# A graph layer summed over half blocks of 128 edges in place of blocks of 256

## The chip, the cores and the metric

One core of a Trainium2 chip runs the whole program. The metric is the device time of one execution in microseconds (us).

## The reference

Four layers follow each other on 3125 nodes with 256 values each: a graph layer over 103,125 edges (three steps), a mixture of experts, a second graph layer over the same edges with 500 relation kinds, and a second mixture of experts. The change is in the second graph layer. The edges come sorted by their target `dst`. Cut to what matters here:

```python
h_src = h_hc[src]                       # one row of 256 values for each edge
r_uv  = r_hc[edge_type]                 # its relation's row
m = clifford_linear(h_src * r_uv, msg_w, msg_b)
m = m * gate[:, :, None] * norm[:, None, None]
h_agg = segment_sum(m, dst, num_segments=num_nodes)
```

Since the linear map is the same for all edges, the kernel sums the products `h_src * r_uv` (already scaled by gate and norm, with the scale itself as column 257) over the edges of a target first, and applies the map to the 3125 sums afterwards.

## The kernel before

The sum is made by `aggregate` (L547). The nodes stand in 25 tiles of 128 (`NT`), and `acc` holds one [128, 257] float32 tile of sums for each, with a 26th as a bin for what belongs to nobody. The 103,424 edge rows are cut into 404 blocks of 256 (`BLOCKS`), in order of `dst`. A block begins in one tile of nodes, whose number is in the table `b_tile`; edges of a block that belong to the next tile are dealt with by 24 more blocks (`EDGES_AT`), one for each border between two tiles: the block in which tile j begins is taken once more with j as its tile. So `total` is 428 blocks.

For each block n, in slot n % 12 (`SLOTS`):

- SP loads the 256 relation rows (L594), 2 rows to a partition, 2080 contiguous bytes each. `relation_rows` was written by earlier stages.
- POOL gathers the 256 rows of `h_table` by two indirect DMAs of 128 rows (L608), with the row numbers in `b_src`. SP and POOL wait until the sum of block n-12 is made, and so run up to 12 blocks ahead.
- ACT makes two one-hot matrices [128 edges, 128 nodes] from `b_near` (L575 twice, L578), in `BANKS` = 6 buffers.
- DVE's queue reads the tile number into a register (L637, `value_load`), DVE multiplies gathered rows by relation rows (L629, 128x514), then adds the sum of block n-3 (`LAG` = 3) from its PSUM bank to `acc[tile]` (L623).
- PE multiplies one-hot by rows, for both halves into one bank (L657): `start` on the first, `stop` on the second, four matmul records of 128x257 in the profile for a block.

Semaphores set the order: `s_sum` counts finished sums (from 13), `s_acc` counts additions (from 6), `s_ready` multiplications, `s_oh` one-hot pairs. The queue of each engine is in the order of the code. DVE's loop is

```python
block_of(n): wait s_rel, s_rows of the slot; multiply; then add(n)
add(g): wait s_acc >= g + BANKS; wait s_sum >= g + (SLOTS + 2 - LAG); addition; s_acc += 1
```

Beside this, `Beside` (L2283) does small work for each of the 25 node tiles, every 14th block from n = 48 on: four transposes and matmuls on PE, a copy on ACT, two additions on DVE (L2365, L2367).

The tables `b_src`, `b_near`, `b_tile` and `b_start` are made early in the program by `edge_blocks` (L361), beside the first relation rows' fetch and store (POOL and ACT's queue, `RelationRows`), and are loaded again much later. `edge_blocks` transposes the edge lists with PE (L465) and picks the 24 border blocks with small matmuls (L470).

## Time and profile before

| | |
|---|---|
| median of 3 runs | 3487.85 us |
| lowest, highest | 3473.99, 3497.01 us |
| the profiled execution's time | 3479.88 us |
| its span, first to last instruction | 3478.1 us |
| mean granted TensorE clock in it | 0.840 |
| busy share PE, DVE, ACT, POOL | 72%, 39%, 41%, 58% |
| DMA moved | 620.94 MB, mean 179 GB/s |

The span is what the trace shows; 1.8 us of the execution lie around it. The busy shares are means over stages that differ in what limits them. The stage of the change runs from 1764 to 2901 us of the span, a third of it. Times in the rows are microseconds from the span's start unless marked ns. Register, branch and semaphore instructions of an engine's queue ("DVEq", "SPq") are not counted as busy.

### The profile page before, as it was taken

How to read it: one execution, taken by the hardware profiler on the slowest of the kernel's cores; microseconds unless marked ns; L12 is line 12 of the kernel's file. 1: busy time of each engine (PE TensorE's matmuls, PEld its weight loads, DVE VectorE, ACT ScalarE, POOL GpSimd, SP SyncE). 2: the span in 40 equal slices, each digit the busy share in tenths (PEclk: the TensorE clock that was granted, in tenths of full speed). 3: DMA queues.
4: the chain of work that ended last, by engine and by line, in shares of the span. 5: the costliest groups of instructions: out<-in, count | busy, mean ns of one | idle time of the engine just before them, and what ended most of it. 6: DMA issues, size and time to landing. Idle time of an engine off the chain costs nothing. (4 is left out here: it accounts for less than half of the span.)

```text
span 3478.1 us, 51218 instructions
## 1 busy us (share of the span) xinstructions
PE 2500.1 (72%) x14080; PEld 1914.7 (55%) x14080; DVE 1343.8 (39%) x4118; ACT 1441.6 (41%) x3690; POOL 2011.4 (58%) x1969
## 2 busy tenths in 40 slices
PE   0156899999999947887036666666666667499997
PEld 0123666678888836776024444444444445488986
DVE  4166889952221142000643444444444435500100
ACT  0025666647650022332354444444444443255553
POOL 0353777777777226663657777777777772033332
PEclk9998999999999958998557667666766768699998
DMA  2574766678888335565367777777777772364232
GB/s 112 191 251 126 209 202 206 206 226 257 269 257 244 123 119 186 181 208 171 104 186 203 202 198 202 202 205 204 206 203 201 205 201 61 124 179 131 37 84 62
DMA packets 314743, 620.94 MB, mean 179 GB/s; under 512 B 82206, under 2 KB 128685, under 8 KB 309777
## 3 DMA queue, kind: packets, MB, share of 16 engines
q1 hardware_dynamic: 207409, 343.11, 30.1%
q0 software_dynamic: 101360, 268.76, 29.2%
q10 hardware_dynamic: 5728, 6.11, 0.5%
q8 instruction: 115, 1.88, 0.2%
q14 instruction: 131, 1.07, 0.1%
HBM read 451.74 MB, written 170.90 MB: 179 GB/s over the span
## 5 line engine op out<-in xcount | busy, mean ns | idle before, releaser
L608 POOL DMA_INDIRECT agg_r_rows<-h_table,parts_and_x x856 | 869.1, 1015 | 296.1 <-issue 218.8
L657 PE MATMUL agg_r_sums<-agg_r_rows,agg_r_onehot 128*128 128x257 f32 x1712 | 703.2, 559 | 389.8 <-DVE agg_r_rows L629 343.6
L657 PEld LDWEIGHTS agg_r_sums<-agg_r_rows,agg_r_onehot 128*128 128x128 f32 x1712 | 430.4, 275 | 645.4 <-issue 581.5
L1412 POOL DMA_INDIRECT rl_buf<-r_table,kinds x608 | 634.4, 1043 | 249.3 <-issue 170.4
L629 DVE TENSOR_TENSOR agg_r_rows<-agg_r_rows,agg_r_rel 128x514 f32<-128x514 f32 x428 | 298.5, 697 | 657.6 <-DMA agg_r_rows<-h_table,parts_and_x 655.6
L575 ACT ACTIVATE agg_r_gap<-iota,parts_and_x 128x128 f32<-128x128 f32 x856 | 295.1, 392 | 496.5 <-PE agg_r_sums L657 470.9
L1782 PE MATMUL f_pH<-f_xT,f_w 128*128 128x128 f32 x2816 | 359.4, 287 | 74.5 <-DMA f_w<-in_L_ffn_w 52.9
L1782 PEld LDWEIGHTS f_pH<-f_xT,f_w 128*128 128x128 f32 x2816 | 343.8, 201 | 106.2 <-DMA f_w<-in_L_ffn_w 57.7
L1134 PE MATMUL ly_acc<-parts,matrix 128*128 128x256 bf16 x1250 | 342.0, 274 | 0.0
L1133 PE MATMUL ly_acc<-parts,matrix 128*128 128x256 bf16 x1250 | 340.2, 272 | 0.0
L1132 PE MATMUL ly_acc<-parts,matrix 128*128 128x257 bf16 (+1 forms) x1250 | 340.0, 272 | 0.0
L1867 ACT ACTIVATE f_hT<-f_pH,f_b 128x128 f32<-128x128 f32 x704 | 197.6, 372 | 333.7 <-PE f_pH L1782 333.4
L1801 PE MATMUL f_pY<-f_w,f_hT 128*128 128x256 f32 x1408 | 327.7, 383 | 0.0
L1801 PEld LDWEIGHTS f_pY<-f_w,f_hT 128*128 128x128 f32 x1408 | 262.0, 193 | 31.4
L2020 POOL DMA_INDIRECT f_xb<-xn_table,f_token x120 | 118.8, 990 | 240.0 <-DVE f_home L1968 116.3
L1270 DVE TENSOR_SCALAR b_oh<-b_numbers,b_code 128x400 bf16<-128x400 f16 x980 | 255.0, 324 | 0.0
L2008 POOL DMA_INDIRECT f_ys<-f_yb,f_home x56 | 88.2, 1575 | 284.3 <-DVE f_yb L1993 242.2
L1121 PE MATMUL b_strips<-b_oh,b_at 128*128 128x400 bf16 x980 | 201.0, 336 | 59.5 <-DVE b_oh L1270 53.5
L1412 POOL DMA_INDIRECT f_rr_buf<-r_table,kinds x120 | 121.4, 1012 | 150.9 <-POOLq L113 112.9
L578 ACT ACTIVATE agg_r_onehot<-agg_r_gap 128x256 f32<-128x256 f32 x428 | 178.2, 416 | 13.5
L623 DVE TENSOR_TENSOR acc<-acc,agg_r_sums 128x257 f32 (+1 forms) x431 | 179.1, 416 | 9.9 <-PE agg_r_sums L657 9.9
L1134 PE MATMUL ly_acc<-parts_and_x,matrix 128*128 128x256 bf16 x625 | 170.6, 273 | 0.0
(394 smaller groups left out, 3404.2 us busy)
## 6 DMA issues: line engine op xcount, KB each, us to landing
agg_r_rel<-relation_rows SPq DMA_DIRECT2D x428, 260.0 KB, 3.0
relation_rows<-rl_buf SPq DMA_DIRECT2D x304, 260.0 KB, 4.5
f_w<-in_L_ffn_W SPq DMA_DIRECT2D x28, 1024.0 KB, 5.0
f_w<-in_L_ffn_w SPq DMA_DIRECT2D x38, 512.0 KB, 5.8
relation_rows<-f_rr_buf POOLq DMA_DIRECT2D x60, 260.0 KB, 2.8
agg_r_rows<-h_table,parts_and_x POOLq DMA_INDIRECT x856, 3.4
ly_zin<-zh SPq DMA_DIRECT2D x50, 256.0 KB, 4.8
zh<-ly_out SPq DMA_DIRECT2D x50, 256.0 KB, 2.7
```

What stands on the lines that cost most here:

```text
L575: last = nc.scalar.activation(gap[:, n % BANKS, t, :], c.iota[:, 0:P], ACT.Abs, bias=c.tab["b_near"][:, bass.ds(g * 2 + t, 1)])
L608: pool.indirect_dma_start(rows[:, n % SLOTS, t, :], None, table, bass.IndirectOffsetOnAxis(ap=indices[:, t:t + 1], axis=0)).then_inc(s_row ...
L629: v.tensor_tensor(here, here, rel[:, n % SLOTS, :, 0:used], ALU.mult).then_inc(s_ready, 1)
L657: last = nc.tensor.matmul(sums[:, n % BANKS, 0:used], onehot[:, n % BANKS, t, :], rows[:, n % SLOTS, t, 0:used], start=t == 0, stop=t == 1)
L1121: last = nc.tensor.matmul(strips[:, n % BANKS, 0:CODES], at[:, n % 2, t, :], oh[:, n % 2, t, :], start=t == 0, stop=t == DEEP - 1)
L1132: nc.tensor.matmul(acc[:, n % 2, 0:D + one], m[:, s, own], of[:, s, 2 * D:3 * D + one], start=s == 0, stop=False)
L1133: nc.tensor.matmul(acc[:, n % 2, 0:D], m[:, s, own], of[:, s, 0:D], start=False, stop=False)
L1134: last = nc.tensor.matmul(acc[:, n % 2, 0:D], m[:, s, own], of[:, s, D:2 * D], start=False, stop=s == NT - 1)
L1270: last = v.tensor_scalar(oh[:, n % 2, t, :], numbers[:, :], code[:, q, 1, own, t:t + 1], None, ALU.is_equal)
L1412: pool.indirect_dma_start(self.buf[:, n, g, :], None, self.table, bass.IndirectOffsetOnAxis(ap=self.c.kinds[:, at:at + 1], axis=0)).then_i ...
L1782: last = nc.tensor.matmul(pH[s][:, f * P:(f + 1) * P], w1b[:, s, h, f * P:(f + 1) * P], xT[:, s, h, :], start=h == 0, stop=h == KD - 1)
L1801: last = nc.tensor.matmul(pY[s][:, 0:D], hT[:, s, f, :], w2b[:, s, f, :], start=f == 0, stop=f == FC - 1)
```

## The change

A half block of 128 edges becomes the unit of the tables, of the one-hot base, of the PSUM bank and of the addition. There are 808 halves, each with a tile number of its own, and 24 halves more for the borders, two of which make one block: `total` is 404 + 12 = 416. Each half's matmul goes to a bank of its own, and DVE adds two banks for each block, with two tile numbers read after the multiplication. Six banks hold three blocks, `LAG` is 2 blocks; the one-hot buffers keep their number, 6 (`HOT`). The relation rows of a block are loaded 128 rows to each half: 1040 contiguous bytes for each partition and half; for the last 12 blocks there are two loads with a start each. `edge_blocks` makes the tables in the new form. Left out of the diff: renamed buffers, and the shapes of tables where they are declared and loaded.

```diff
-SLOTS, BANKS, LAG = 12, 6, 3
+SLOTS, BANKS, LAG, HOT = 12, 6, 2, 6
+HALVES, PER_HALF = 2 * BLOCKS, 2 * PER_PART
@@ edge_blocks: vector
-                v.tensor_scalar(at[:, 0, :], starts, block_bits, block_bits, ALU.arith_shift_right, ALU.logical_shift_left)
+                v.tensor_scalar(at[:, 0, :], starts, bits, bits, ALU.arith_shift_right, ALU.logical_shift_left)
...
-                for b in range(PER_PART):
+                for b in range(PER_HALF):
                     last = v.tensor_scalar(pick[:, b, :], own[:, :], float(b), None, ALU.is_equal)
...
-                for q in range(2):
-                    v.tensor_copy(src_out[:, BLOCKS:, q], extra[:, q * 32:q * 32 + EDGES_AT])
-                    last = v.tensor_tensor(near_out[:, BLOCKS:, q], shift[:, :], extra[:, 64 + q * 32:64 + q * 32 + EDGES_AT], ALU.subtract)
-                last.then_inc(s_out, 1)
+                v.tensor_copy(src_out[:, HALVES:], extra[:, 0:EDGES_AT])
+                v.tensor_tensor(near_out[:, HALVES:], shift[:, :], extra[:, 32:32 + EDGES_AT], ALU.subtract).then_inc(s_out, 1)
@@ edge_blocks: tensor
-                for q in range(4):
-                    for b in range(PER_PART):
-                        last = nc.tensor.matmul(extra[:, q * 32:q * 32 + EDGES_AT], both[:, q // 2, b, q % 2:BLOCK:2], pick[:, b, :],
-                                                start=b == 0, stop=b == PER_PART - 1)
+                for q in range(2):
+                    for b in range(PER_HALF):
+                        last = nc.tensor.matmul(extra[:, q * 32:q * 32 + EDGES_AT], both[:, q, b, :], pick[:, b, :],
+                                                start=b == 0, stop=b == PER_HALF - 1)
@@ aggregate
-    total = BLOCKS + EDGES_AT
+    total = BLOCKS + EDGES_AT // 2
@@ aggregate: scalar
-                    act.wait_ge(s_sum, g + (SLOTS + 2 - BANKS))
+                    act.wait_ge(s_sum, g + (SLOTS + 2 - HOT))
@@ aggregate: sync
-                def relation(n, start):
-                    sp.wait_ge(s_sum, (n + 2))
-                    src = relation_rows[bass.ds(start, BLOCK), :].rearrange("(p k) c -> p (k c)", p=P)
-                    sp.dma_start(rel[:, n % SLOTS, :, :].rearrange("p k c -> p (k c)"), src).then_inc(s_rel[n % SLOTS], 16)
                 for n in range(BLOCKS):
-                    relation(n, n * BLOCK)
+                    sp.wait_ge(s_sum, n + 2)
+                    src = relation_rows[n * BLOCK:(n + 1) * BLOCK, :].rearrange("(k p) c -> p k c", p=P)
+                    sp.dma_start(rel[:, n % SLOTS, :, :], src).then_inc(s_rel[n % SLOTS], 16)
                 for n in range(BLOCKS, total):
-                    relation(n, sp.value_load(c.tab["b_start"][0:1, n - BLOCKS:n - BLOCKS + 1], min_val=0, max_val=EDGE_TILES * P))
+                    starts = [sp.value_load(c.tab["b_start"][0:1, at:at + 1], min_val=0, max_val=EDGE_TILES * P)
+                              for at in (2 * (n - BLOCKS), 2 * (n - BLOCKS) + 1)]
+                    sp.wait_ge(s_sum, n + 2)
+                    for t in range(2):
+                        sp.dma_start(rel[:, n % SLOTS, t, :], relation_rows[bass.ds(starts[t], P), :]).then_inc(s_rel[n % SLOTS], 16)
@@ aggregate: vector
+                def add(n):
+                    tiles = [tile_of(2 * (n - LAG) + t) for t in range(2)]
+                    dve.wait_ge(s_sum, n + (SLOTS + 2 - LAG))
+                    for t in range(2):
+                        dve.wait_ge(s_acc, 2 * n + t + BANKS)
+                        here = acc[:, bass.ds(tiles[t], 1), 0:used].rearrange("p a d -> p (a d)")
+                        v.tensor_tensor(here, here, sums[:, (2 * (n - LAG) + t) % BANKS, 0:used], ALU.add).then_inc(s_acc, 1)
...
                 for n in range(total):
-                    if n - LAG < BLOCKS:
-                        tile = dve.value_load(c.tab["b_tile"][0:1, n:n + 1], min_val=0, max_val=NT)
-                    else:
-                        tile = n - LAG - BLOCKS + 1
-                    block_of(n, n, n // SLOTS + 1, tile)
+                    dve.wait_ge(s_rel[n % SLOTS], loads_of(n))
+                    dve.wait_ge(s_rows[n % SLOTS], (n // SLOTS + 1) * 32)
+                    here = rows[:, n % SLOTS, :, 0:used]
+                    v.tensor_tensor(here, here, rel[:, n % SLOTS, :, 0:used], ALU.mult).then_inc(s_ready, 1)
+                    add(n)
                     beside.vector(dve, v, n)
@@ aggregate: tensor
-                    pe.wait_ge(s_acc, g + (LAG + 1))
+                    pe.wait_ge(s_acc, 2 * (g + LAG + 1))
...
-                        last = nc.tensor.matmul(sums[:, n % BANKS, 0:used], onehot[:, n % BANKS, t, :], rows[:, n % SLOTS, t, 0:used],
-                                                start=t == 0, stop=t == 1)
+                        last = nc.tensor.matmul(sums[:, (2 * n + t) % BANKS, 0:used], onehot[:, n % HOT, t, :], rows[:, n % SLOTS, t, 0:used],
+                                                start=True, stop=True)
```

`tile_of(half)` is a `value_load` of `b_tile` for the 808 halves, and a constant for the 24 border halves.

## Rows read from the trace of the kernel before

**Rows 1.** Page, costliest groups: operation xcount | busy us, mean ns | idle before, releaser.
```profile
...
L608 POOL DMA_INDIRECT agg_r_rows<-h_table,parts_and_x x856 | 869.1, 1015 | 296.1 <-issue 218.8
L657 PE MATMUL agg_r_sums<-agg_r_rows,agg_r_onehot 128*128 128x257 f32 x1712 | 703.2, 559 | 389.8 <-DVE agg_r_rows L629 343.6
...
L629 DVE TENSOR_TENSOR agg_r_rows<-agg_r_rows,agg_r_rel 128x514 f32<-128x514 f32 x428 | 298.5, 697 | 657.6 <-DMA agg_r_rows<-h_table,parts_and_x 655.6
L575 ACT ACTIVATE agg_r_gap<-iota,parts_and_x 128x128 f32<-128x128 f32 x856 | 295.1, 392 | 496.5 <-PE agg_r_sums L657 470.9
...
L623 DVE TENSOR_TENSOR acc<-acc,agg_r_sums 128x257 f32 (+1 forms) x431 | 179.1, 416 | 9.9 <-PE agg_r_sums L657 9.9
...
```
**Rows 2.** Busy time of each engine in the stage, granted TensorE clock, DMA share, GB/s.
```profile
...
1766.00:2900.00 1134.00, 745.16 (x1880) 474.64 (x1880) 466.15 (x911) 483.25 (x1345) 869.01 (x856) 0.69 0.72 202
...
```
**Rows 3.** The gathers' line, L608: min/median/max ns, first and last start; waits; landing.
```profile
...
L608 POOL DMA_INDIRECT agg_r_rows<-h_table,parts_and_x x856: 949/953/1470, 1765.9 to 2894.7; - x172
...
  issue: 218.8, 718
  PE agg_r_sums L657: 41.8, 137
...
DMA to landing us min/median/max: 2.7/3.4/6.0
```
**Rows 4.** Timeline of POOL, 2005 to 2013.5 us: start, duration, operation, idle before it.
```profile
...
2005.16 1.40 POOL L608 DMA_INDIRECT agg_r_rows<-h_table,parts_and_x  x1 [0.30 <-issue]
...
2011.10 0.96 POOL L608 DMA_INDIRECT agg_r_rows<-h_table,parts_and_x  x1 [0.30 <-PE agg_r_sums L657]
...
```
**Rows 5.** Timeline of DVE in the same stretch.
```profile
...
2005.05 0.70 DVE L629 TENSOR_TENSOR agg_r_rows<-agg_r_rows,agg_r_rel 128x514 f32<-128x514 f32 x1 [1.96 <-DMA agg_r_rows<-h_table,parts_and_x]
...
2010.31 0.70 DVE L629 TENSOR_TENSOR agg_r_rows<-agg_r_rows,agg_r_rel 128x514 f32<-128x514 f32 x1 [1.26 <-DMA agg_r_rows<-h_table,parts_and_x]
2010.92 0.41 DVE L623 TENSOR_TENSOR acc<-acc,agg_r_sums 128x257 f32 x1
...
```
**Rows 6.** Timeline of DVE where it catches up, 1788 to 1797.5 us.
```profile
...
1789.73 0.42 DVE L623 TENSOR_TENSOR acc<-acc,agg_r_sums 128x257 f32 x1 [7.68 <-PE agg_r_sums L657]
...
1795.03 0.70 DVE L629 TENSOR_TENSOR agg_r_rows<-agg_r_rows,agg_r_rel 128x514 f32<-128x514 f32 x1
1795.64 0.42 DVE L623 TENSOR_TENSOR acc<-acc,agg_r_sums 128x257 f32 x1
1795.97 0.69 DVE L629 TENSOR_TENSOR agg_r_rows<-agg_r_rows,agg_r_rel 128x514 f32<-128x514 f32 x1
...
```
**Rows 7.** Line L637, reading of the tile number by DVE's queue (ns min/median/max).
```profile
...
L637 DVEq TENSOR_LOAD <-b_tile x407: 298/304/327, 1771.4 to 2840.9; - x136
L637 DVEq FUSED_REGOPS  x407: 190/190/190, 1771.7 to 2841.2; - x136
L637 DVEq SEQ_ASSERT  x407: 23/23/33, 1772.0 to 2841.5; - x136
...
```
**Rows 8.** Timeline of DVE at the end of the stage.
```profile
...
2898.12 1.33 DVE L623 TENSOR_TENSOR acc<-acc,agg_r_sums 128x257 f32<-128x257 f32 x3
2900.51 0.42 DVE L623 TENSOR_TENSOR acc<-acc,agg_r_sums 128x257 f32<-128x257 f32 x1 [1.06 <-PE agg_r_sums L657]
```
**Rows 9.** Groups of the stage by line: one of the two additions of Beside.
```profile
...
L2367 DVE TENSOR_TENSOR parts_and_x<-parts_and_x,upd_bias 128x256 f32<-128x256 f32 x25 | 10.6, 424 | 0.9
...
```
**Rows 10.** DMA queues, 2000 to 2600 us: packets, MB, share of 16 engines.
```profile
...
q0 software_dynamic: 21858, 60.62, 38.5%
q1 hardware_dynamic: 32802, 60.68, 33.3%
...
```
**Rows 11.** DMA queues, 1758.5 to 1766 us, where 1040-byte rows are stored alone.
```profile
...
q1 hardware_dynamic: 656, 0.67, 25.4%
...
```
**Rows 12.** End of the stage that makes the tables: last POOL start, last SP issue.
```profile
...
179.37 0.95 POOL L1412 DMA_INDIRECT re_buf<-r_table,kinds  x1 [0.30 <-issue]
...
```
**Rows 13.** The same stage, SP's queue.
```profile
...
174.19 0.43 SPq L411 DMA_DIRECT2D b_near_d<-eb_near  x1
```

More of the change, by code:

```diff
@@ L463, in _ @@
                     for b in range(PER_PART):
-                        src = both[:, 0, b, q % 2:BLOCK:2] if q < 2 else near[:, 0, b, q % 2:BLOCK:2]
+                        half = (q % 2) * PER_PART + b
+                        src = both[:, 0, half, :] if q < 2 else near[:, half, :]
                         last = nc.tensor.transpose(turned[:, q, b * PARTS:(b + 1) * PARTS], src, c.ident[0:PARTS, 0:PARTS])
@@ L571, in places @@
                     g = n
-                    act.wait_ge(s_sum, g + (SLOTS + 2 - BANKS))
+                    act.wait_ge(s_sum, g + (SLOTS + 2 - HOT))
                     for t in range(2):
-                        last = nc.scalar.activation(gap[:, n % BANKS, t, :], c.iota[:, 0:P], ACT.Abs, bias=c.tab["b_near"][:, bass.ds(g * 2 + t, 1)])
+                        last = nc.scalar.activation(gap[:, n % HOT, t, :], c.iota[:, 0:P], ACT.Abs, bias=c.tab["b_near"][:, bass.ds(g * 2 + t, 1)])
                     last.then_inc(s_gap, 1)
                     act.wait_ge(s_gap, g + 1)
-                    nc.scalar.activation(onehot[:, n % BANKS, :, :], gap[:, n % BANKS, :, :], ACT.Relu, bias=1.0, scale=-1.0).then_inc(s_oh, 1)
+                    nc.scalar.activation(onehot[:, n % HOT, :, :], gap[:, n % HOT, :, :], ACT.Relu, bias=1.0, scale=-1.0).then_inc(s_oh, 1)
                 for n in range(total):
@@ L616, in _, with loads_of, tile_of @@
                 v = nc.vector
-                def add(g, bank, tile):
-                    dve.wait_ge(s_acc, g + BANKS)
-                    dve.wait_ge(s_sum, g + (SLOTS + 2 - LAG))
-                    here = acc[:, bass.ds(tile, 1), 0:used].rearrange("p a d -> p (a d)")
-                    v.tensor_tensor(here, here, sums[:, bank, 0:used], ALU.add).then_inc(s_acc, 1)
-                def block_of(g, n, uses, tile):
-                    dve.wait_ge(s_rel[n % SLOTS], uses * 16)
-                    dve.wait_ge(s_rows[n % SLOTS], uses * 32)
-                    here = rows[:, n % SLOTS, :, 0:used]
-                    v.tensor_tensor(here, here, rel[:, n % SLOTS, :, 0:used], ALU.mult).then_inc(s_ready, 1)
-                    add(g, (n - LAG) % BANKS, tile)
-                v.memset(c.tab["b_tile"][:, 0:LAG], NT).then_inc(s_acc, 1)
+                def loads_of(n):
+                    slot = [q for q in range(n + 1) if q % SLOTS == n % SLOTS]
+                    return sum(16 if q < BLOCKS else 32 for q in slot)
+                def tile_of(half):
+                    at = half + 2 * LAG
+                    return dve.value_load(c.tab["b_tile"][0:1, at:at + 1], min_val=0, max_val=NT) if half < HALVES else half - HALVES + 1
+                def add(n):
[5 more added lines that the diff above has]
+                        v.tensor_tensor(here, here, sums[:, (2 * (n - LAG) + t) % BANKS, 0:used], ALU.add).then_inc(s_acc, 1)
+                v.memset(c.tab["b_tile"][:, 0:2 * LAG], NT).then_inc(s_acc, 1)
                 v.memset(acc[:, :, :], 0.0).then_inc(s_acc, BANKS - 1)
```

49 lines of the change are left out of this document (24 added, 25 removed).

## The prediction

> **What bounds the kernel now.** The first view is the page's list of groups [rows 1]: the costliest line is L608, the gathers of the second graph layer, 856 of them with 869.1 us on POOL. The second view is the table of busy time for the stage [rows 2]: POOL is busy 869 of 1134 us, PE 745, ACT 483, DVE 466, the DMA engines 0.72. No engine is full by its busy time, so the question is what fills POOL's gaps. The third view is the gathers' line by itself [rows 3]: 718 of the gaps are "issue", 0.30 us each (218.8/718), and the 137 put down to PE are 0.31 each (41.8/137), the same gap; one of that kind stands in the timeline, 0.30 [rows 4]. A real wait for a free slot would have all lengths. So POOL never waits for the others after the first gather: it goes from one gather to the next with 0.30 us between. The first starts at 1765.9 and the last at 2894.7, 1128.8/855 = 1.320 us apart, 2.640 us a block of two. The layer's time is the number of gathers by that pace. DVE shows the reverse: idle 657.6 us, of which 655.6 for landing gathers, and PE waits for DVE [rows 1].
>
> The pace has two parts. The median gather takes 0.953 us, which with the gap makes 1.255; the mean is 1.015 [rows 1, 3]. The timelines side by side show the difference: the gather at 2005.16 takes 1.40 us while DVE's multiplication from 2005.05 to 2005.75 is under way; the one at 2011.10 takes 0.96, though DVE's addition of 2010.92 overlaps it [rows 4, 5]. A gather that starts under the multiplication (two inputs in SBUF) waits for its end; an addition, whose one input is in PSUM, costs nothing. In all (1.015 - 0.953) x 856 = 53 us of the stage are this.
>
> The Trainium skill (SBUF — State Buffer, section "Who interferes with whom") states that a VectorE instruction with two SBUF inputs contends with a GpSimd instruction that reads SBUF, and that one with at most one SBUF input, outside the 2-port modes, does not. By it too the new additions, PSUM plus SBUF, are free for POOL. Its remark there that tensor_tensor was not seen to stall DMA would make the 53 us something else; the two timelines speak against that.
>
> **The change part by part.** *Fewer blocks.* 428 become 416, so 24 gathers go: 24 x 1.320 = 31.7 us. This is on the path as long as POOL sets the pace.
>
> *The second addition and the second reading of a tile number, on DVE.* DVE has slack, and the question is how much is left. Where DVE catches up, its multiplications start 0.94 us apart (1795.03, 1795.97) with one reading and one addition between [rows 6]. The reading's three queue steps are 304 + 190 + 23 = 517 ns [rows 7]; they run while the multiplication is being executed, since 0.70 + 0.42 + 0.52 would be 1.64. In the new loop both readings stand behind the multiplication and ahead of both additions, so they no longer hide behind an addition. Each costs at least 0.52 us, and at most 0.94, which holds a whole loop; I take 0.65, near the low end, because the 0.94 also holds a multiplication, an addition and their waits. Then the wait and the address: 0.1 to 0.3, an estimate from the register step of 0.19 [rows 7]; I take 0.2. The second addition waits for the first by `s_acc`: three that follow one another so take 1.33 us, 0.44 each [rows 8]; with an address to be worked out between them up to 0.19 more; I take 0.55. The next multiplication starts 0.33 us after the last addition's start (1795.64 to 1795.97). Sum, from one multiplication to the next: 1.30 + 0.20 + 0.55 + 0.33 = 2.38 us, with ends 1.04 + 0.10 + 0.44 + 0.33 = 1.9 and 1.88 + 0.30 + 0.63 + 0.44 = 3.25. Every 14th block Beside adds two additions of 0.42 [rows 9], 0.85 us, 25 times 21 us, 0.05 a block. So DVE needs 2.43 where POOL gives 2.51 at its barest and 2.64 in the mean: covered, but with a tenth to spare and no longer by half. What is queued behind DVE's waits is the next multiplication; PE and, 12 blocks later, POOL and SP wait for it. If the cover is gone the price is the rival below.
>
> *When the multiplications come.* The 53 us hang on where they fall among the gathers. DVE starts some 6 blocks behind: PE's first sums come late (DVE idles 7.68 us until 1789.73 [rows 6]), POOL has issued (1789.7 - 1765.9)/2.64 = 9 blocks by then, and with a lag of 2 DVE has multiplied 3. It catches up at only 0.2 us a block, and later, too, two multiplications can't come nearer than 2.38 us. At a fixed distance just under POOL's 2.51 they drift slowly past the gathers and one hit pushes POOL out of reach for some blocks. The loss can fall to none (gain 53), or grow if each block is hit, up to the longest excess of 1.470 - 0.953 = 0.52 us for 416 blocks, 215 less 53. At 2.38 the drift of 0.13 brings the next hit after some four blocks, and 0.5/4 is no less than the 0.13 a block of now; only in the narrow band of 2.45 to 2.51 does it pay. I take 8 us gained, near no change.
>
> *The relation rows in 1040-byte pieces.* Now q1 takes 33.3% of 16 engines for 60.68 MB, that is 0.333 x 16 x 600 = 3197 us, 52.7 us a MB, at 2080 bytes apiece; the gathers take 38.5% [rows 10]. Where 1040-byte rows are stored alone, 656 packets of 0.67 MB take 0.254 x 16 x 7.5 = 30.5 us, 46.5 ns each, 45.5 us a MB [rows 11]. So a half piece costs about half, and the share stays near 0.72. The upper end is that each piece costs what a whole one does: 33.3% more, 105%, and the engines would be the bound. I take 0, hidden by the 12 slots ahead.
>
> The Trainium skill (DMA: Bandwidth & Descriptors, section "How a descriptor splits into AXI transactions") says that a piece that doesn't start at a multiple of 256 bytes also fetches the bytes before its start. With about 4 extra beats of 32 bytes for each start, an estimate from that page, two pieces need 73 beats for 69, 6% more on q1, a share of 0.74 for 0.72: nothing on the time either.
>
> *The rest.* PE has the same four records a block; its new bound for `s_acc` asks for the additions of block g-3, which stand ahead of the multiplication g that it waits for anyway. ACT's two Abs and one Relu are as before, with six buffers still. SP reads two starts and issues two loads in the last 12 blocks only, under 2.5 us each and 12 blocks ahead. The stage ends with one more addition behind the last sum: +0.45 [rows 8]. `edge_blocks` has 4 more small DVE operations and 2 fewer, the same 16 + 16 matmuls; its last save is issued at 174.2, while POOL's beside it starts its last gather at 179.4 [rows 12, 13], so 5 us hide what is at most 1.
>
> Sum against the profiled execution: -31.7 - 8 + 0.5 = -39, from 3479.9 to 3441. The median of the runs is 8.0 us above the profiled one; I set the forecast on the median's scale: 3487.85 - 39 = 3449.
>
> **The rivals.** *DVE in step with POOL.* If DVE's distance is 2.45 to 2.51, most of the 53 us goes as well. For: the sum 2.43 is near. Against: it needs a window of 0.06. With two thirds gone: -31.7 - 35 = -67, 3421.
>
> *DVE's queue becomes the bound, mildly or plainly.* DVE starts its run at about 1790 with 401 multiplications before the last 12 left, so the stage ends near 1790 + 401 D + 19 (12 at 1.6, without readings) + 21 (Beside) + 4 (from the last multiplication to the last addition). It ends at 2900.9 now, so the break-even is D = 2.66 us. For D between 2.55 and 2.66 the gain is 44 to 0; I price it at 2.62: -16, 3472. Above it the change is slower: at 2.8 us the end is 2957, +56, 3544. Against: all middle values would have to be off to the same side by 0.3. For: the upper end is 3.25, and no row shows two readings in a row.
>
> On the readings, the Trainium skill (DMA: Bandwidth & Descriptors, section "Latency and other measured facts") puts the floor of a tensor_load at about 600 ns. By that, two of them would add 0.6 us to D, 2.98, and the result would be 3616. The 407 loads of this trace take 298 to 327 ns [rows 7], so that case gets 1 in 100, inside the slower one.
>
> *The DMA engines become the bound.* At 105% a block takes 2.77 us, 416 x 2.77 = 1152 for 1130: +22, 3510. Rows 11 speak against it.
>
> *The change doesn't do what it says for the time:* were the gathers not what sets the end, 24 fewer of them would save nothing, 3488. The even gap of 0.30 speaks against that.
>
> **How the numbers follow.** Chances: forecast (2.38 covered, 3434 to 3462) 0.50; in step 0.22; DVE mildly the bound 0.13; DVE plainly the bound 0.06; DMA 0.04; no change 0.05. The range 3408 to 3482 takes in the first three down to 80 us gained, with 0.15 left out. A measurement of this kernel can tell some 1%, 35 us, from no change. Faster by more than 1%: three fifths of the forecast's half, all of "in step", a little of the mild case, 0.54. Slower by more: 0.06. Same: 0.40.
>
> **What would show it.** Right: 832 gathers, gaps of 0.30 us, 1.27 to 1.32 us apart, the last started near 2857; DVE's smallest distance near 2.4 where it catches up; its idle time for landings down from 656 to under 300. Gather durations fall towards 0.953 in the mean if it is in step. DVE the bound: POOL's gaps grow beyond 0.30 towards PE, and DVE waits for nothing. DMA: a share near 1, landings far above 3.4. The prediction is wrong if a reading of a tile number costs more behind the multiplication than its three steps, or if the drift brings more hits than now.

## The result and the profile after

| | before | changed kernel |
|---|---|---|
| median of 9 runs on one chip | 3481.2 us (3471.0 to 3497.0) | 3455.9 us (3447.6 to 3460.6) |
| ratio, with 95% interval | | 0.9922 [0.9900, 0.9943] |
| profiled execution, span | 3479.9, 3478.1 us | 3447.6, 3445.9 us |
| mean granted TensorE clock | 0.840 | 0.842 |

The ratio is worth 27 us (0.0078 x 3481), the spans differ by 32.2 us. In the interval's terms the gain is 20 to 35 us: small, but there, and at the edge of what the prediction called measurable.

The costliest groups of the page, changed kernel: operation xcount | busy us, mean ns | idle before, releaser.

```profile
L607 POOL DMA_INDIRECT agg_r_rows<-h_table,parts_and_x x832 | 848.5, 1020 | 289.5 <-issue 213.7
...
L633 DVE TENSOR_TENSOR acc<-acc,agg_r_sums 128x257 f32 (+1 forms) x836 | 353.5, 423 | 353.9 <-issue 245.8
...
L642 DVE TENSOR_TENSOR agg_r_rows<-agg_r_rows,agg_r_rel 128x514 f32<-128x514 f32 x416 | 289.5, 696 | 101.4 <-DMA agg_r_rows<-h_table,parts_and_x 97.8
```

L607, L660, L633, L642 and L623 (further down) are the lines L608, L657, L623, L629 and L637 of [rows 1]. The reader is to see three things. The gathers are 832 and a mean one takes 1020 ns, where it was 1015. The additions have about doubled (179.1 us to 353.5). DVE's idle time for landing gathers has gone from 655.6 us to 97.8: most of its waiting for rows is gone, and that alone cost no time here.

The gathers' line by itself, changed kernel (durations, then what POOL sat idle for, then who waited for the gathers):

```profile
L607 POOL DMA_INDIRECT agg_r_rows<-h_table,parts_and_x x832: 949/953/1469, 1762.6 to 2863.5; - x167
...
  issue: 213.7, 701
  PE agg_r_sums L660: 39.6, 130
...
  DVE agg_r_rows L642: 97.8, 171
...
DMA to landing us min/median/max: 2.7/3.4/6.4
```

Beside [rows 3] this is the account of the result. Gaps are 0.30 us again, by either name (213.7/701, 39.6/130), so POOL still waits for nobody after its first gather. The first gather to the last takes 1100.9 us for 1128.8: 27.9 less. By count, 24 gathers at 1.320 are 31.7; by pace, 1100.9/831 = 1.3248 for 1.3203, 831 gathers give 3.7 back. The other 4 us of the spans' difference lie outside: the stage starts 3.3 us earlier (1762.6 for 1765.9), in work that the change hardly touches, and I can't give a cause for that.

One line of the table of busy time for the stage (1764 to 2870), changed kernel: window, length, then PE, PEld, DVE, ACT, POOL busy, granted clock, DMA share, GB/s.

```profile
1764.00:2870.00 1106.00, 733.45 (x1832) 452.22 (x1832) 649.85 (x1305) 471.30 (x1309) 847.45 (x831) 0.69 0.72 202
```

Against [rows 2]: DVE 466 to 650, the rest a little less, clock 0.69 and DMA 0.72 unchanged. The relation rows' DMA queue between 2000 and 2600, changed kernel (packets, MB, share of 16 engines):

```profile
q1 hardware_dynamic: 61956, 60.65, 35.1%
```

q1 has nearly twice the packets of [rows 10] for the same MB, and its share is 35.1% for 33.3%: by the same working, 55.6 us a MB for 52.7. The half pieces cost 5% more on a queue that isn't the bound.

What DVE does where it catches up, changed kernel (start, length, idle before it):

```profile
1791.99 0.69 DVE L642 TENSOR_TENSOR agg_r_rows<-agg_r_rows,agg_r_rel 128x514 f32<-128x514 f32 x1
1793.21 1.00 DVE L633 TENSOR_TENSOR acc<-acc,agg_r_sums 128x257 f32 x2 [0.53 <-issue]
1794.13 0.69 DVE L642 TENSOR_TENSOR agg_r_rows<-agg_r_rows,agg_r_rel 128x514 f32<-128x514 f32 x1
1795.35 1.00 DVE L633 TENSOR_TENSOR acc<-acc,agg_r_sums 128x257 f32 x2 [0.54 <-issue]
1796.27 0.69 DVE L642 TENSOR_TENSOR agg_r_rows<-agg_r_rows,agg_r_rel 128x514 f32<-128x514 f32 x1
```

From one multiplication to the next it is 2.14 us (1791.99, 1794.13, 1796.27): 1.22 to the first addition, in which both readings pass, and 0.92 from there to the next multiplication. That is the distance while DVE catches up; for a multiplication that had to wait for its rows it is longer (below). The three steps of a reading, changed kernel (ns, min/median/max):

```profile
L623 DVEq TENSOR_LOAD <-b_tile x812: 296/303/340, 1770.1 to 2842.3; - x163
L623 DVEq FUSED_REGOPS  x812: 190/190/190, 1770.4 to 2842.7; - x163
L623 DVEq SEQ_ASSERT  x812: 23/23/33, 1770.7 to 2842.9; - x163
```

They are those of [rows 7], twice as many; 1.22/2 = 0.61 is what a reading costs here, with its steps of 0.52. One reading more adds 0.61 as well (e6).

Gathers and multiplications in the middle of the stage, changed kernel, PE's lines left out:

```profile
2008.05 0.70 DVE L642 TENSOR_TENSOR agg_r_rows<-agg_r_rows,agg_r_rel 128x514 f32<-128x514 f32 x1
2008.41 1.15 POOL L607 DMA_INDIRECT agg_r_rows<-h_table,parts_and_x  x1 [0.30 <-issue]
...
2009.51 0.99 DVE L633 TENSOR_TENSOR acc<-acc,agg_r_sums 128x257 f32 x2 [0.77 <-issue]
2009.87 0.95 POOL L607 DMA_INDIRECT agg_r_rows<-h_table,parts_and_x  x1 [0.30 <-issue]
2011.10 0.75 DVE L642 TENSOR_TENSOR agg_r_rows<-agg_r_rows,agg_r_rel 128x514 f32<-128x514 f32 x1 [0.60 <-DMA agg_r_rows<-h_table,parts_and_x]
2011.13 0.96 POOL L607 DMA_INDIRECT agg_r_rows<-h_table,parts_and_x  x1 [0.30 <-issue]
```

The gather at 2008.41 begins under a multiplication, which ends at 2008.75, and takes 1.15. The one at 2009.87 begins under two additions and takes 0.95. The one at 2011.13 starts with the multiplication, 0.03 us after it, and takes 0.96: what costs is to begin well inside one. The multiplication at 2011.10 waited for a landing, as 171 of the 416 do by the gathers' line: these begin when rows land, not at a fixed distance from the last. Behind a multiplication that had waited, the first addition starts 1.46 us later (2008.05 to 2009.51) and not 1.22: here the first load starts with the multiplication (2008.07 for 2008.05), in the catch-up ahead of it, while the last addition is still being executed (1793.92 for 1794.13). With the 0.92 behind it the next multiplication can then come after 2.38 us. Among the blocks 10 to 403 the trace has 214 with 1.40 to 1.52 and 136 with 1.18 to 1.30.

The end of the stage, changed kernel:

```profile
...
2869.28 0.88 DVE L633 TENSOR_TENSOR acc<-acc,agg_r_sums 128x257 f32<-128x257 f32 x2 [0.47 <-PE agg_r_sums L660]
```

The last additions end at 2870.2, 6.7 us behind the start of the last gather; it was 6.2 (2894.7, and 2900.51 with its addition [rows 3, 8]). That is the one addition more.

### The profile page after: what moved, and what is told of

It is laid out like the page before. It is cut to its first block and busy times, and to the rows that moved or that the text cites. A ratio compares the mean times of both kernels' runs of the same rounds, so it can differ in the third digit from the quotient of the medians.

```text
span 3445.9 us, 53030 instructions
## 1 busy us (share of the span) xinstructions
PE 2485.3 (72%) x14033; PEld 1889.3 (55%) x14033; DVE 1527.7 (44%) x4513; ACT 1429.9 (41%) x3654; POOL 1988.4 (58%) x1945
## 5 line engine op out<-in xcount | busy, mean ns | idle before, releaser
L607 POOL DMA_INDIRECT agg_r_rows<-h_table,parts_and_x x832 | 848.5, 1020 | 289.5 <-issue 213.7
L660 PE MATMUL agg_r_sums<-agg_r_rows,agg_r_onehot 128*128 128x257 f32 x1664 | 692.7, 559 | 374.0 <-DVE agg_r_rows L642 309.2
L660 PEld LDWEIGHTS agg_r_sums<-agg_r_rows,agg_r_onehot 128*128 128x128 f32 x1664 | 411.3, 272 | 642.4 <-issue 348.3
L633 DVE TENSOR_TENSOR acc<-acc,agg_r_sums 128x257 f32 (+1 forms) x836 | 353.5, 423 | 353.9 <-issue 245.8
L574 ACT ACTIVATE agg_r_gap<-iota,parts_and_x 128x128 f32<-128x128 f32 x832 | 287.0, 392 | 496.5 <-PE agg_r_sums L660 470.1
L642 DVE TENSOR_TENSOR agg_r_rows<-agg_r_rows,agg_r_rel 128x514 f32<-128x514 f32 x416 | 289.5, 696 | 101.4 <-DMA agg_r_rows<-h_table,parts_and_x 97.8
L1415 POOL DMA_INDIRECT f_rr_buf<-r_table,kinds x120 | 121.4, 1012 | 150.0 <-POOLq L114 112.0
L1990 DVE TENSOR_TENSOR f_plain<-f_pY,f_b 128x256 f32<-128x256 f32 x56 | 23.8, 425 | 369.4 <-PE f_pY L1804 369.4
```

Source lines behind the costliest of these rows:

```text
L574: last = nc.scalar.activation(gap[:, n % HOT, t, :], c.iota[:, 0:P], ACT.Abs, bias=c.tab["b_near"][:, bass.ds(g * 2 + t, 1)])
L607: pool.indirect_dma_start(rows[:, n % SLOTS, t, :], None, table, bass.IndirectOffsetOnAxis(ap=indices[:, t:t + 1], axis=0)).then_inc(s_row ...
L633: v.tensor_tensor(here, here, sums[:, (2 * (n - LAG) + t) % BANKS, 0:used], ALU.add).then_inc(s_acc, 1)
L642: v.tensor_tensor(here, here, rel[:, n % SLOTS, :, 0:used], ALU.mult).then_inc(s_ready, 1)
L660: last = nc.tensor.matmul(sums[:, (2 * n + t) % BANKS, 0:used], onehot[:, n % HOT, t, :], rows[:, n % SLOTS, t, 0:used], start=True, stop= ...
L1415: pool.indirect_dma_start(self.buf[:, n, g, :], None, self.table, bass.IndirectOffsetOnAxis(ap=self.c.kinds[:, at:at + 1], axis=0)).then_i ...
```

## The experiments

The kernels ran on four chips, A to D (which chip gave the first result is not on record, so D may be the same). On A, B and C the kernel before itself takes 4010 to 4066 us, on D and in the first result 3478 to 3481; each kernel is therefore compared with the kernel before on its own chip. "First to last" is from the start of the first gather to that of the last, from the gathers' line of each trace.

| chip, before's median | kernel | ratio [95%] | gathers, mean ns | first to last, us | a gather, us |
|---|---|---|---|---|---|
| first result, 3481.2 | before | 1 | 856, 1015 | 1128.8 | 1.320 |
| | changed | 0.9922 [0.9900, 0.9943] | 832, 1020 | 1100.9 | 1.325 |
| D, 3478.2 | e11, before, lag 2 | 1.0003 [0.9990, 1.0016] | 856, 1015 | 1128.7 | 1.320 |
| | e12, changed, lag 3 | 0.9933 [0.9916, 0.9950] | 832, 1024 | 1104.2 | 1.329 |
| A, 4021.1 | e1, before, 416 blocks | 0.9894 [0.9833, 0.9954] | 832, 1004 | 1203.5 | 1.448 |
| | e2, before, 1040-byte pieces | 1.0003 [0.9975, 1.0030] | 856, 1010 | 1233.1 | 1.442 |
| | e3, before, PSUM factor | 1.0011 [0.9986, 1.0036] | 856, 953 | 1240.1 | 1.450 |
| | e4, changed, 428 blocks | 1.0207 [1.0158, 1.0255] | 856, 1011 | 1321.6 | 1.546 |
| B, 4010.4 | e5, changed, spacer | 1.0163 [1.0102, 1.0225] | 832, 987 | 1297.1 | 1.561 |
| | e6, changed, third reading | 1.0200 [1.0131, 1.0268] | 832, 986 | 1309.1 | 1.575 |
| C, 4066.0 | e7, before, one run | | 856, 1005 | 1251.0 | 1.463 |
| | e8, changed | 1.0103 [1.0013, 1.0192] | 832, 1012 | 1296.8 | 1.561 |
| | e9, changed, interleaved | 1.0132 [1.0046, 1.0218] | 832, 1052 | 1286.1 | 1.548 |
| | e10, changed, readings first | 1.0183 [1.0108, 1.0258] | 832, 974 | 1305.6 | 1.571 |

### One part at a time (chip A)

**e1_before_416**: the kernel before, with only the number of blocks cut. Its last 12 border blocks are left out.

```diff
-    total = BLOCKS + EDGES_AT
+    total = BLOCKS + EDGES_AT // 2
```

> The kernel before with 12 border blocks left out (416 blocks in place of 428, nothing else; the last 12 borders are left out of the sums). Theory (the gathers' number by their pace is the layer's time): 24 gathers at 1.320 us go, the stage is 31.7 us shorter, pace per gather still 1.32 us, ratio 0.991. Rival (the end is set by something else than the number of gathers): less than 10 us, ratio 0.998 or more.

The ratio is 0.9894 [0.9833, 0.9954], 18 to 67 us less; the medians, 3991.8 and 4021.1, differ by 29. The first gather to the last is 29.6 us shorter than in e2, which has the same loop and all blocks; 24 gathers at e2's 1.442 are 34.6. So the count is worth what the count times the pace says, on this chip too.

**e2_before_pieces**: only the relation rows in 1040-byte pieces.

```diff
-                    src = relation_rows[bass.ds(start, BLOCK), :].rearrange("(p k) c -> p (k c)", p=P)
-                    sp.dma_start(rel[:, n % SLOTS, :, :].rearrange("p k c -> p (k c)"), src).then_inc(s_rel[n % SLOTS], 16)
+                    src = relation_rows[bass.ds(start, BLOCK), :].rearrange("(k p) c -> p k c", p=P)
+                    sp.dma_start(rel[:, n % SLOTS, :, :], src).then_inc(s_rel[n % SLOTS], 16)
```

> The kernel before with the relation rows loaded in 1040-byte pieces as in the changed kernel, 128 rows to each half (so they don't match the gathered rows of the blocks, which still go two to a partition). Theory (pieces are hidden): q1's share of the stage within 2 points of 33.3%, gathers 1.015 us in the mean, no change, ratio 0.999 to 1.001. Rival (the pieces slow the gathers' landing and move the multiplications onto the gathers): gathers 1.02 us or more, some 4 us slower or more, up to 22 us.

Ratio 1.0003 [0.9975, 1.0030]. The DMA queue from 2300 to 3300, first of e1 (whole pieces), then of e2:

```profile
q1 hardware_dynamic: 49401, 91.36, 29.0%
```

```profile
q1 hardware_dynamic: 92885, 90.93, 30.6%
```

Nearly twice the packets, 1.6 points of share: 50.8 us a MB (0.290 x 16 x 1000 / 91.36) become 53.8, 6% more. The pieces are hidden; the DMA rival is out.

**e3_before_psum_mult**: the multiplication's second factor is a PSUM bank filled with ones, in place of the relation rows, which are loaded and not used. One bank of the six goes to it.

```diff
-SLOTS, BANKS, LAG = 12, 6, 3
+SLOTS, BANKS, LAG = 12, 5, 3
...
-                    v.tensor_tensor(here, here, rel[:, n % SLOTS, :, 0:used], ALU.mult).then_inc(s_ready, 1)
+                    v.tensor_tensor(here, here, bc(unit[:, 0:1, 0:used], [P, 2, used]), ALU.mult).then_inc(s_ready, 1)
```

> The kernel before with the multiplication by the relation rows replaced by one by ones from a PSUM bank, of the same 128x514 size (5 banks for the sums in place of 6; the relation rows are loaded and not used). Theory (gathers wait for an instruction of DVE with two SBUF inputs): every gather takes 0.95 us, mean 0.953 for 1.015, pace 1.255 us, the stage is 53 us shorter, ratio 0.985. Rival (the excess comes from the DMA rings or from memory): mean still 1.01 or more, no change.

The gathers' group of the page, first e2, then e3:

```profile
L608 POOL DMA_INDIRECT agg_r_rows<-h_table,parts_and_x x856 | 864.2, 1010 | 418.7 <-issue 243.3
```

```profile
L609 POOL DMA_INDIRECT agg_r_rows<-h_table,parts_and_x x856 | 816.1, 953 | 473.7 <-issue 246.2
```

The mean falls from 1010 to 953 ns, which is the median: the whole excess is gone when the multiplication has only one input in SBUF. Four gathers of the 856 still take over 1.0 us, up to 1204 ns, and all four begin under the second addition of `Beside`, whose two inputs are in SBUF. That shows the mechanism that the prediction read from two timelines. The time did not move (1.0011 [0.9986, 1.0036]), against an expected ratio of 0.985: POOL is busy 48 us less and idle 55 us more (418.7 to 473.7). On this chip POOL is not the bound, so what the 53 us are worth where it is was not measured.

**e4_after_428**: the changed kernel with 12 blocks more, which repeat its last border block and add to the bin.

```diff
-    total = BLOCKS + EDGES_AT // 2
+    real = BLOCKS + EDGES_AT // 2
+    total = real + 12
...
```

> The changed kernel with 12 blocks more at the end, which repeat the last block and add to the bin (428 blocks). Theory: 24 gathers at 1.325 us come back, 31.8 us slower than the changed kernel, so within 5 us of the kernel before, ratio 1.000 to 1.002. Rival (the change also gained or lost elsewhere by its halves): a time 10 us or more away from before.

It took 4107.5 us, ratio 1.0207 [1.0158, 1.0255], where the count alone would have made it equal to before. This miss was the first sign that the half-block form has a price of its own, on this chip. The gathers' line of e4:

```profile
L608 POOL DMA_INDIRECT agg_r_rows<-h_table,parts_and_x x856: 951/957/1474, 2180.5 to 3502.1; - x172
...
  issue: 225.9, 717
  PE agg_r_sums L661: 204.7, 124
```

Those 124 waits for PE are 1.65 us each: real waits for a free slot, unlike the 0.30 of the first result. With 856 gathers in both, e4 needs 88 us more than e2 from the first to the last.

### The distance of DVE's multiplications (chips B and C)

The rival was that DVE's smallest distance from one multiplication to the next, D (not the chip D), decides. It is 2.14 us in the changed kernel's catch-up. Four kernels move it.

**e5_after_spacer**: one more DVE operation, with a PSUM input, between the readings and the first addition.

```diff
...
+                        if t == 0:
+                            v.tensor_tensor(spare[:, :], acc[:, NT, 0:257], sums[:, (2 * (n - LAG) + t) % BANKS, 0:257], ALU.mult)
```

> The changed kernel with one needless instruction of DVE more in each block, a 128x257 multiplication with one PSUM input between the readings and the first addition. Theory (where the multiplications fall decides the gathers' excess, and DVE's smallest distance of 2.14 us grows by about 0.34 to 2.48, 2.54 with Beside, in step with POOL's bare 2.51): the gathers' mean falls from 1.020 towards 0.97, the stage is 20 to 40 us shorter than the changed kernel's although DVE does more. Rival A (phase plays no part): nothing changes, within 5 us of the changed kernel. Rival B (DVE is then the bound): up to 10 us slower than the changed kernel, with waits of POOL beyond 0.30 us.

**e6_after_third_reading**: the first tile number is read once more.

```diff
                     tiles = [tile_of(2 * (n - LAG) + t) for t in range(2)]
+                    tile_of(2 * (n - LAG))
```

> The changed kernel with a third, unused reading of a tile number in each block. Theory (a reading behind the multiplication costs its three steps and their gaps, 0.61 us, and DVE's smallest distance goes from 2.14 to 2.75): DVE becomes the bound, the stage ends at 1787 + 401 x 2.75 + 44 = 2934 in place of 2870, 64 us slower than the changed kernel, some 35 us slower than the kernel before; POOL waits for slots. Rival (readings run ahead of the additions and cost nothing): the time of the changed kernel.

e5: D is 2.36 us (multiplications at 2417.73, 2420.08, 2422.45), ratio 1.0163 [1.0102, 1.0225]. e6: D is 2.75 (2414.73, 2417.50, 2420.24, 2423.00), ratio 1.0200 [1.0131, 1.0268]. A reading more is 2.75 - 2.14 = 0.61 again. Since POOL waited for slots in both (193.6 and 202.5 us for PE in the gathers' line), no phase between multiplications and an unbroken run of gathers exists here: the rival "in step with POOL" was not tested. Nor did the changed kernel itself run on B, so what either edit adds to its time is not measured.

The next four went to one chip, with both kernels unchanged beside them. **e7_before_again** and **e8_after_again**:

> The kernel before itself, unchanged, for a profile of the chip on which the experiments run. If that chip has it at some 4010 us, theory (late semaphores: other engines see PE's sums some microseconds late, and DVE then catches up): DVE's multiplications come in bursts 0.94 us apart between gaps of 4 to 8 us, POOL waits for slots for some 100 us, and the layer takes some 1235 us for 1130. If it has it at 3480: the rows of the trace before.

> The changed kernel itself, unchanged, on the chip of the experiments. Theory where the chip has the kernel before at some 4010 us: DVE catches up at 2.14 us a block in place of 0.94, so that the 12 slots run empty and POOL waits: 20 to 60 us slower than the kernel before although 24 gathers are gone, ratio 1.005 to 1.015. Rival (the number of gathers counts here too): ratio 0.99, as for the kernel before without 12 blocks. Where the chip has it at 3480: ratio 0.992.

The change costs 1.03% here, 1.0103 [1.0013, 1.0192], where it gains 0.8% on the first chip. The gathers' line of e7:

```profile
L608 POOL DMA_INDIRECT agg_r_rows<-h_table,parts_and_x x856: 947/953/1470, 2233.2 to 3484.2; - x172
...
  issue: 239.7, 758
  DMA b_rec<-records: 122.1, 54
...
  PE agg_r_sums L657: 30.2, 43
```

and of e8:

```profile
L607 POOL DMA_INDIRECT agg_r_rows<-h_table,parts_and_x x832: 947/953/1474, 2232.7 to 3529.5; - x167
...
  issue: 220.4, 675
  PE agg_r_sums L660: 202.1, 137
...
  DMA b_rec<-records: 33.2, 19
```

"b_rec<-records" is a load of a much earlier stage: the releaser is wrongly named, and what POOL waits for is a slot. The gather itself is as in the first result, 953 in the median. It is the waits that are new, 54 long ones of 2.3 us (122.1/54) in the kernel before. DVE's timeline of e7 shows what happens around one:

```profile
2605.64 0.70 DVE L629 TENSOR_TENSOR agg_r_rows<-agg_r_rows,agg_r_rel 128x514 f32<-128x514 f32 x1 [0.30 <-issue]
2615.46 0.42 DVE L623 TENSOR_TENSOR acc<-acc,agg_r_sums 128x257 f32 x1 [9.13 <-DMA b_rec<-records]
2616.18 0.70 DVE L629 TENSOR_TENSOR agg_r_rows<-agg_r_rows,agg_r_rel 128x514 f32<-128x514 f32 x1 [0.30 <-issue]
...
2617.13 0.70 DVE L629 TENSOR_TENSOR agg_r_rows<-agg_r_rows,agg_r_rel 128x514 f32<-128x514 f32 x1
```

and DVE's timeline of e8:

```profile
2607.99 0.99 DVE L633 TENSOR_TENSOR acc<-acc,agg_r_sums 128x257 f32 x2 [3.60 <-issue]
...
2611.32 0.99 DVE L633 TENSOR_TENSOR acc<-acc,agg_r_sums 128x257 f32 x2 [1.73 <-issue]
2612.23 0.69 DVE L642 TENSOR_TENSOR agg_r_rows<-agg_r_rows,agg_r_rel 128x514 f32<-128x514 f32 x1
...
2614.36 0.69 DVE L642 TENSOR_TENSOR agg_r_rows<-agg_r_rows,agg_r_rel 128x514 f32<-128x514 f32 x1
...
2616.49 0.69 DVE L642 TENSOR_TENSOR agg_r_rows<-agg_r_rows,agg_r_rel 128x514 f32<-128x514 f32 x1
```

A hole of 9 us opens in DVE's work in e7, and the backlog is then worked off at 0.95 us a block; in e8 it is worked off at 2.13. What the engines wait for is seen in e1 (chip A), where PE and the engines behind it stand in one timeline:

```profile
2479.20 2.05 PE L657 MATMUL agg_r_sums<-agg_r_rows,agg_r_onehot 128*128 128x257 f32 x4 [0.45 <-ACT agg_r_onehot L578]
2483.35 2.05 PE L657 MATMUL agg_r_sums<-agg_r_rows,agg_r_onehot 128*128 128x257 f32 x4 [2.10 <-DVE agg_r_rows L629]
...
2497.03 2.05 PE L657 MATMUL agg_r_sums<-agg_r_rows,agg_r_onehot 128*128 128x257 f32 x4 [6.55 <-issue]
...
2505.09 0.33 SPq L594 DMA_DIRECT2D agg_r_rel<-relation_rows  x1
2505.09 0.69 ACT L575 ACTIVATE agg_r_gap<-iota,parts_and_x 128x128 f32<-128x128 f32 x2 [8.67 <-DMA b_rec<-records]
2505.27 0.42 DVE L623 TENSOR_TENSOR acc<-acc,agg_r_sums 128x257 f32 x1 [8.39 <-DMA b_rec<-records]
...
2505.85 0.95 POOL L608 DMA_INDIRECT agg_r_rows<-h_table,parts_and_x  x1 [2.80 <-DMA b_rec<-records]
```

PE's last matmul before the hole ends by its record at 2499.1, and all four engines that wait for a sum go on together at 2505.1 to 2505.9. The sum that they wait for isn't this last one. DVE's addition at 2505.27 follows the multiplication of 2496.19, whose own block PE sums at 2497.03, and by the program it adds the sum of three blocks before: the one of 2479.20, which ends by its record at 2481.25. ACT, SP and POOL, counted by block, stand where their program waits for this same sum. So it is seen 24 us after its recorded end. PE has summed three more blocks since (from 2483.35, 2489.35 and 2497.03), so by its records it is not the sum that was late but the news of it.

A second thing is slow on these chips: at times DVE's queue. The last of a reading's three steps takes 23/23/33 ns in [rows 7] and in the changed kernel of the first result. In e7 and then in e8 it is (ns, min/median/max):

```profile
L637 DVEq SEQ_ASSERT  x407: 1/23/728, 2239.3 to 3440.6; - x136
```

```profile
L623 DVEq SEQ_ASSERT  x812: 1/23/723, 2241.4 to 3532.9; - x163
```

In some stretches each instruction of this queue takes about 0.7 us, whichever it is: in e10 eight in a row between 2407.9 and 2414.3, while DVE executes nothing for 5.9 us. Other records beside such ones have 1 or 2 ns, so it is the stretch that tells, and not the single record. Between the first gather and the last, records of 0.67 to 0.74 us are 70 of 2481 in e7 and 416 of 4047 in e8, and none in the first result (the longest is 0.34). All records of this queue together take 294 us in e7, where the kernel before of the first result has 252, and 683 in e8 for 489.

**e9_after_interleaved**: the second tile number is read between the two additions. **e10_after_readings_first**: both are read ahead of the multiplication.

```diff
-                    tiles = [tile_of(2 * (n - LAG) + t) for t in range(2)]
-                    dve.wait_ge(s_sum, n + (SLOTS + 2 - LAG))
                     for t in range(2):
+                        tile = tile_of(2 * (n - LAG) + t)
+                        if t == 0:
+                            dve.wait_ge(s_sum, n + (SLOTS + 2 - LAG))
```

```diff
-                def add(n):
+                def add(n, tiles):
-                    tiles = [tile_of(2 * (n - LAG) + t) for t in range(2)]
...
                 for n in range(total):
+                    tiles = [tile_of(2 * (n - LAG) + t) for t in range(2)]
                     dve.wait_ge(s_rel[n % SLOTS], loads_of(n))
...
-                    add(n)
+                    add(n, tiles)
...
```

> The changed kernel with the second tile number read between the two additions in place of ahead of both. Theory (the sequence of readings and additions sets DVE's smallest distance): the first reading hides behind the multiplication, the second beside the first addition, distance 1.87 us for 2.14; where the chip has the kernel before at 3480 no change against the changed kernel, at 4010 some 10 to 20 us faster than the changed kernel. Rival (a reading costs 0.61 wherever it stands): distance 2.14.

> The changed kernel with both readings ahead of the multiplication. Theory: the readings start when the second addition has been issued, 1.24 us, then the multiplication, and the second addition waits for the first: distance 2.45 to 2.5 us, longer than the 2.14 of the changed kernel; the time is that of the changed kernel at 3480, and 10 us or more slower at 4010. In step with POOL's 2.51 there may be fewer hits: gathers 0.98 in the mean. Rival: distance 2.14 or less.

e9's D is 1.70 us (multiplications at 2421.78, 2423.47, 2425.18, 2426.87), e10's 2.52 (2416.36, 2418.88, 2421.40). The ratios are 1.0132 [1.0046, 1.0218] and 1.0183 [1.0108, 1.0258], with e8's 1.0103 [1.0013, 1.0192] between them and no change: the three intervals overlap. From the first gather to the last it is 1286.1, 1296.8 and 1305.6 us at D = 1.70, 2.13 and 2.52. That is 24 us for 1 us of D, and points to D having some effect. On chip B e5 and e6 differ by 12.0 us for 0.39 us of D, which is 31 for 1; all these are single traces. It doesn't explain the change's cost: with e7's pace, 831 gathers would take 1216 us, e8 needs 81 more, and from 2.13 down to the 0.94 of the kernel before this slope gives 29. e9, at 1.70, still needs 70 more. Of the expected distances e6's (2.75) came true and e10's nearly (2.45 to 2.5); 1.87 was expected for e9, and 2.48 for e5, which has 2.36. That e9 would be 10 to 20 us faster than the changed kernel is neither shown nor refuted.

### The lag (chip D)

Two things besides D differ: the banks a half block each, and the lag of two blocks instead of three. **e11_before_lag2** is the kernel before with `LAG` 2; **e12_after_lag3** the changed kernel with `LAG` 3 over the same six banks.

```diff
-SLOTS, BANKS, LAG = 12, 6, 3
+SLOTS, BANKS, LAG = 12, 6, 2
```

```diff
-SLOTS, BANKS, LAG, HOT = 12, 6, 2, 6
+SLOTS, BANKS, LAG, HOT = 12, 6, 3, 6
-... and LAG < BANKS // 2
+... and LAG <= BANKS // 2
```

> The kernel before with LAG = 2 in place of 3 (DVE adds the sum of block n-2 after the multiplication n), nothing else. On a chip that has the kernel before at some 4010 to 4070 us: theory (late semaphores are met by the lag: with two blocks between multiplication and addition each delay of PE's sum reaches DVE, and the changed kernel loses there by its lag) ratio 1.01 to 1.02. Rival (DVE's smallest distance, 0.94 us here as before, is what loses): ratio 0.998 to 1.003. On a chip that has it at 3480: no change by either.

> The changed kernel with LAG = 3 over the same six banks: DVE adds block n-3 after the multiplication n, and PE's sum n waits for these two additions, since it takes their banks. On a chip that has the kernel before at some 4010 to 4070 us: theory (the lag) 10 to 30 us faster than the changed kernel, ratio to before 0.99 to 1.003. Rival (DVE's distance, still 2.14, or PE's later start): 1.008 or more. On a chip that has it at 3480: POOL's pace as before, ratio 0.99 to 0.993, so that it would be the version that beats both.

This chip was one where the kernel before takes 3478 us. There e11 is 1.0003 [0.9990, 1.0016], and e12 is 0.9933 [0.9916, 0.9950], the changed kernel's ratio within the intervals. The gathers' group of the page in e12:

```profile
L607 POOL DMA_INDIRECT agg_r_rows<-h_table,parts_and_x x832 | 851.8, 1024 | 290.0 <-issue 243.9
```

With POOL unbroken, one block of lag more or less is worth nothing. It is also a second series in which the half-block form gains, 23 us (0.0067 x 3478.2). For the chips with holes the lag is untried. None of the versions beats both kernels: e12 can't be told from the change, and e1 leaves blocks out.

## Why the prediction was right, and where it was off

The forecast was 3449 us on the scale of the first median, 39 below it; measured are 27 by the ratio, 32 by the spans. The time of 3455.9 is in the range, 7 us above the forecast; that the forecast took 7 to 12 us too much is partly hidden by its starting point, the median of three runs, 6.7 above that of nine.

- *The bound, and fewer blocks (-31.7).* Right. POOL's gaps are 0.30 in the changed kernel, its last gather starts at 2863.5 (2857 was forecast; by its own sum it would be 2855), and 24 gathers by the pace are the gain. e1 has it by itself.
- *When the multiplications come (-8).* The step that was mis-sized. The excess went from (1.015 - 0.953) x 856 = 53 to (1.020 - 0.953) x 832 = 56 us: +3, not -8; a pace of 1.3248 where 1.320 stood costs 3.7. The mechanism is right, and e3 shows it: no two-SBUF-input multiplication, no excess. What was wrong is the picture of multiplications that follow each other at DVE's smallest distance once it is busy. 171 of the 416 still wait for rows to land (before it was 415 of 428), and the rest follow at 2.14, 2.38 or more, so that their places among the gathers keep changing. Gathers over 0.97 us are 198 of 832, where they were 192 of 856. Why that gives just as many hits as before was not tried by itself.
- *D = 2.38.* There are two distances. Where DVE catches up, which is what the prediction's sum is for, it is 2.14: the readings are 0.61 each (0.65 taken), there is no 0.20 for the wait and the address ahead of the first addition, and from the first addition to the next multiplication it is 0.92 (0.88 taken). Behind a multiplication that had waited for its rows it is 1.46 + 0.92 = 2.38; that this is the forecast's number is luck, since no term of the sum stands for it. With 2.14 the drift against POOL's 2.51 is 0.37 us a block and not 0.13; "in step with POOL" needs 0.07 us more than 2.38 and 0.31 more than 2.14. With 2.66 as the break-even, "DVE the bound" needed 0.3 to 0.5 more.
- *The half pieces (0).* Right: 5% and 6% more on q1, nothing on the time (e2). The estimate by the Trainium skill (DMA: Bandwidth & Descriptors, section "How a descriptor splits into AXI transactions") was 6% more on q1; both traces agree.
- *The tail (+0.5).* Right, 0.43.
- *PE, ACT, SP, `edge_blocks` (0).* No row shows a cost. The stage starts 3.3 us earlier and not later.
- *Two dear readings (3616).* Not seen: a load takes 303 ns in the median and a whole reading 0.61 us, so the measurement decides against the 600 ns for the load alone. (On chips A to C some loads take 0.7 us, in the stretches in which the whole queue is slow; their median is 301 to 303 in e7 and e8.)

What no part of the prediction had is that the answer depends on the chip. The argument was made from a trace in which POOL never waits, and it holds in both series where that is so. On the three others the same program has holes (on B only the changed form was traced), POOL waits for slots, and the half-block form, which in the first result costs 3.7 us, costs 81 to 88 us of the stage (e8 against e7's pace, e4 against e2), more than the 35 that 24 gathers bring. In the prediction's words, "covered, but with a tenth to spare" was no price there, and what the spare had been good for was not asked.

How the 81 to 88 divide is open. D accounts for some 29 by the slope of e8 to e10, if that is more than scatter. The rest would fall to the lag, to the banks or to the slow queue. In the changed kernel the multiplication n stands behind the sum of n-3, in the kernel before behind that of n-4, so a sum that is seen late stops DVE, and with it PE, sooner. And it has 1.6 times as many instructions in DVE's queue, which lost 194 us in e8 and 42 in e7 by the slow stretches (683 less 489, 294 less 252). Both are argued only. e11 and e12 would tell of the lag and ran where there are no holes. Against the queue as the only cause stands that e9 has 447 records of some 0.7 us and the shortest stage of the three changed forms on its chip, e10 256 and the longest; no run has fewer queue instructions with the same banks and lag. What makes the sums come late and the queue slow on these chips is open as well, and no run shows whether the recording of the trace has a part in it.

## What to carry to other kernels

Where one engine works through a stage without a real wait, the stage is worth its count of instructions by its pace, and slack that other engines lose costs nothing: look at the gaps' lengths, not at their total. That slack is what makes up for delays, though, so a change that spends it should be timed on a chip where the sums or transfers come late before it is called a gain; the numbers to compare are how fast the engine works off a backlog, here 0.95 us a block and then 2.13, and how many instructions its queue has for a block. For an effect that hangs on when two instructions meet (the multiplication and the start of a gather), take no gain into the sum without a row that shows their new spacing.

## What the runs showed of the hardware

- The same program takes 3478 to 3481 us in two series and 4010 to 4066 on three other chips. Single operations are as fast there (a gather 953 to 957 ns in the median). But engines that wait for PE can go on long after the recorded end of the sum that they need (24 us in e1), and in some stretches each instruction of DVE's queue takes some 0.7 us, also one of 23 ns. In the kernel before the stage is 122 us of the 590 longer (e7); the rest lies ahead of it, above all: it starts at 2233.2 for 1765.9.
- A start of a 128-row gather is held while a 128x514 multiplication with two SBUF inputs is under way (up to 1469 ns for 953), and not by one with a PSUM input (mean 953, e3), nor by additions with a PSUM input.
- Reading a number from SBUF into a register costs DVE's queue 0.61 us each time, beside the operation that DVE executes. The order alone moves the smallest distance of the loop: both ahead of the multiplication 2.52 us, behind it 2.14, one between the additions 1.70. One operation of 0.42 us more between the readings and the first addition adds 0.22 (e5).
